# Feature attention in a two-layer decoder kernel: next maxima turned behind the tenth head, values written by GpSimd from a feature-major context, selu added by GpSimd a turn later

## The reference

```python
x = x + _L0_xattn_ref(_layernorm(x, axis=-1), ctx_2048, ctx_2048, L0_xattn_W)

def _L0_xattn_ref(q, k, v, W):          # q, k, v: (32, 64, 256)
    H, D = 8, 8
    SCALE = D ** (-0.5)
    qh = q.reshape(Bq, H, D, Tq); kh = k.reshape(Bq, H, D, Tk); vh = v.reshape(Bq, H, D, Tk)
    a = jnp.einsum('bhdq,bhdk->bhqk', qh, kh) * SCALE
    p = jax.nn.softmax(a, axis=-1)
    y = jnp.einsum('bhqk,bhdk->bhdq', p, vh).reshape(Bq, Cq, Tq)
    out = jnp.einsum('oc,bct->bot', W, y)
    return jax.nn.selu(out)
```

## Time and profile before

| | us |
|---|---|
| median of 3 runs | 1331.83 |
| lowest and highest | 1327.61 and 1333.07 |
| profiled execution, its time | 1335.5 |
| its span | 1333.4 |
| PE busy | 1217.7 (91%) |
| DVE busy | 959.4 (72%) |
| ACT busy | 709.4 (53%) |
| POOL busy | 454.4 (34%) |

### The profile page before, as it was taken

One profiled execution on the slowest core, in us unless ns is written; L12 is line 12 of the kernel. 1 busy time (PEld: TensorE's weight loads), 2 busy tenths in 40 slices (PEclk: granted clock), 3 DMA queues, 4 the chain that ended last, 5 costly groups with the idle time before them and its releaser, 6 DMA issues. The chain is left out here.

```text
span 1333.4 us, 27527 instructions
## 1 busy us (share of the span) xinstructions
PE 1217.7 (91%) x9976; PEld 967.8 (73%) x9976; DVE 959.4 (72%) x1862; ACT 709.4 (53%) x1475; POOL 454.4 (34%) x537
## 2 busy tenths in 40 slices
PE   5999997989888779798899999999997899999998
PEld 3777764444444557697677878788786899999998
DVE  5889987888887376786567778687775668555555
ACT  2778863878778545000466565656653463333332
POOL 2344642454543124575552423323230201112210
PEclk9999998999999988899999999999999999999999
DMA  5111151133331200001300000000000300000001
GB/s 172 36 36 37 42 149 34 41 81 94 80 92 33 74 41 0 1 0 29 119 9 4 4 8 4 8 4 8 4 1 2 95 25 25 25 25 25 1 1 64
DMA packets 58660, 51.04 MB, mean 38 GB/s; under 512 B 9064, under 2 KB 50888, under 8 KB 58184
## 3 DMA queue, kind: packets, MB, share of 16 engines
q1 hardware_dynamic: 58574, 49.88, 13.3%
HBM read 37.93 MB, written 11.53 MB: 37 GB/s over the span
## 5 line engine op out<-in xcount | busy, mean ns | idle before, releaser
L208 DVE TENSOR_REDUCE stacks_neg_max<-psum 128x2 f32<-128x512 f32 x256 | 163.6, 684 | 39.2 <-PE psum L204 38.6
L952 ACT ACTIVATE fa_probs<-psum 128x1024 f32<-128x1024 f32 x128 | 130.3, 1020 | 46.1 <-PE psum L1069 45.3
L1921 PE MATMUL psum<-mo_xT_high,mo_w_high 128*128 128x256 f32 x512 | 145.2, 284 | 2.8 <-DVE mo_xT_low L2755 2.7
L1921 PE MATMUL psum<-mo_xT_low,mo_w_high 128*128 128x256 f32 x512 | 145.0, 283 | 0.0
L1921 PE MATMUL psum<-mo_xT_high,mo_w_low 128*128 128x256 f32 x512 | 144.2, 282 | 0.0
L2587 ACT ACTIVATE mo_silu<-psum 128x256 f32<-128x256 f32 x128 | 49.0, 384 | 155.0 <-PE psum L1921 155.0
L2721 DVE TENSOR_TENSOR mo_mid<-mo_silu,psum 128x256 f32<-128x256 f32 x128 | 53.6, 419 | 92.9 <-ACT mo_silu L2587 92.8
L204 PE MATMUL psum<-stacks_k_stack,stacks_q_stack 48*128 48x256 bf16 x512 | 89.7, 281 | 16.9 <-DVE stacks_neg_max L208 7.8
L2057 POOL TENSOR_TENSOR ga_probs<-ga_probs,ga_top 128x1024 f32<-128x1024 f32 x16 | 30.5, 1905 | 205.4 <-DVE ga_top L2211 205.4
L1921 PEld LDWEIGHTS psum<-mo_xT_high,mo_w_high 128*128 128x128 f32 x512 | 97.0, 189 | 3.2 <-DVE mo_xT_low L2755 2.8
L1921 PEld LDWEIGHTS psum<-mo_xT_low,mo_w_high 128*128 128x128 f32 x512 | 97.1, 190 | 0.0
(11 more groups left out here) (434 smaller groups left out, 3562.3 us busy)
## 6 DMA issues: line engine op xcount, KB each, us to landing
k_parts<-da_k_parts SPq DMA_DIRECT2D x96, 64.0 KB, 2.0
stacks_k_stack<-k_parts SPq DMA_DIRECT2D x32, 192.0 KB
q_parts<-stacks_parts SPq DMA_DIRECT2D x48, 64.0 KB, 2.0
stacks_q_stack<-q_parts SPq DMA_DIRECT2D x32, 96.0 KB
x<-in_x SPq DMA_DIRECT2D x4, 512.0 KB, 7.4
da_context<-in_ctx SPq DMA_DIRECT2D x4, 512.0 KB, 6.9
stacks_q_stack<-q_parts SPq DMA_DIRECT2D x32, 64.0 KB
fa_context<-in_ctx SPq DMA_DIRECT2D x16, 128.0 KB, 2.1
```

The lines of the kernel that those rows point to most:

```text
L208: return core.nc.vector.tensor_reduce(self.neg_max[:, b, :, head_at(h)], core.psum[:, bank, :].rearrange("p (q k) -> p q k", q=2), AX.X, A ...
L952: nc.scalar.activation(probs[:, g].rearrange("p h k q -> p h (k q)"), ps[:, 2 + 2 * (g % 2):4 + 2 * (g % 2), :], ACT.Exp).then_inc(exp_don ...
L1921: done = nc.tensor.matmul(out, lhsT[i], rhs[j], start=start and k == 0, stop=stop and k == 2)
```

## The change

TensorE turns the next tile's maxima of b=0 directly behind `heads(1, 0)`, that is behind head 9, the tenth; it did so behind `heads(1, 1)` and a mix. The `w_out` product moves from there to behind `turn_mixed(t, 0)`, before `heads(1, 3)`, where the two context transposes were. These are gone: SP loads the context from `ctxT`, feature-major, which another sublayer reads already, and GpSimd writes `values` from it by adding zeros. On ScalarE the maxima's rows are copied right after the first exponential of b=1, and `below`, `above` and `exp_below` stand together before the last exponential. On GpSimd selu of tile t-2 comes first in turn t, where that of tile t-1 stood in its middle; `split` moves from first to behind `values_of`. VectorE's `row_stats` moves from behind heads 4 and 5 to behind heads 8 and 9.

```diff
-                sp.dma_start(context[:, slot], dram["ctx"][bass.ts(tile, P), :]).then_inc(context_ready[slot], 16)
+                sp.dma_start(context[:, slot], chunked(dram["ctxT"])[:, :, bass.ts(tile, P)]).then_inc(context_ready[slot], 16)
...
-                        sp.wait_ge(values_psum, t)
+                        sp.wait_ge(values_ready, t)
...
-                        if g == 2 and b == 0 and valid(t - 2):
+                        if g == 0 and b == 1 and valid(t - 2):
                             row_stats(t - 2)
...
                     exponentials(t, 1, 0)
+                if valid(t + 1):
+                    max_to_rows(t + 1, 0)
+                if valid(t):
+                    exponentials(t, 1, 1)
+                    take_mixed(t, 0)
+                    exponentials(t, 1, 2)
                 if valid(t - 1):
                     act.wait_ge(projected, t)
...
-                if valid(t):
-                    exponentials(t, 1, 1)
-                    take_mixed(t, 0)
-                if valid(t + 1):
-                    max_to_rows(t + 1, 0)
...
-                    values_of(t + 1, ring(1))
...
+            def values_of(tile, slot, round):
+                pool.wait_ge(context_ready[slot], 16 * round + 16)
+                if started(tile, RING):
+                    pool.wait_ge(mixed_done, 4 * (tile - 3))
+                as_values = lambda a: a.rearrange("p k (g d) -> p k g d", d=C_HD)
+                nc.gpsimd.tensor_tensor(values[:, slot, :, :, 0:C_HD], as_values(context[:, slot]),
+                                        as_values(zeros[:].rearrange("p (k f) -> p k f", k=KC)), ALU.add).then_inc(values_ready, 1)
...
+                if valid(t - 2):
+                    add_selu(t - 2)
+                if valid(t + 1):
+                    split_max(t + 1, 0)
...
+                    values_of(t + 1, ring(1), rounds(1))
                 if valid(t + 3) and started(t, 1):
                     split(t + 3, ring(3), rounds(3))
...
                 if valid(t + 1):
                     split_max(t + 1, 1)
+                if isinstance(t, int) and t == TILES:
+                    add_selu(t - 1)
...
                 heads(1, 0)
-                if valid(t - 1):
-                    pe.wait_ge(mixed_c_ready, t)
-                    nc.tensor.matmul(ps[:, 7, E:2 * E], w_out[:], mixed_c[:], start=True, stop=True).then_inc(projected, 1)
-                heads(1, 1)
-                if valid(t):
-                    mix(t, ring(0), 0, 1)
...
                     turn_max(t + 1, 0)
+                heads(1, 1)
+                if valid(t):
+                    mix(t, ring(0), 0, 1)
                 heads(1, 2)
                 if valid(t):
                     turn_mixed(t, 0)
-                if valid(t + 1):
-                    pe.wait_ge(context_ready[ring(1)], 16 * rounds(1) + 16)
-                    pe.wait_ge(max_rows_ready, 2 * t + 3)
-                    for k in range(2):
-                        done = nc.tensor.transpose(ps[:, 7, k * P:(k + 1) * P], context[:, ring(1), k * P:(k + 1) * P], ident[:])
-                    done.then_inc(values_psum, 1)
+                if valid(t - 1):
+                    pe.wait_ge(mixed_c_ready, t)
+                    if valid(t + 1):
+                        pe.wait_ge(max_rows_ready, 2 * t + 3)
+                    nc.tensor.matmul(ps[:, 7, E:2 * E], w_out[:], mixed_c[:], start=True, stop=True).then_inc(projected, 1)
```

More of the change, by code:

```diff
@@ L790, in feature_attention @@
         zeros, parts, q_stack, k_stack = stacks.zeros, stacks.parts, stacks.q_stack, stacks.k_stack
-        context = sb("context", [P, RING, E])
+        context = sb("context", [P, RING, KC, P])
         rest = sb("rest", [P, E])
@@ L938, in _ @@
         def _(act):
-            def values_of(tile, slot):
-                act.wait_ge(values_psum, tile + 1)
-                nc.scalar.copy(values[:, slot, :, :, 0:C_HD],
-                               ps[:, 7, 0:E].rearrange("p (k g d) -> p k g d", k=2, d=C_HD)).then_inc(values_ready, 1)
             def max_to_rows(tile, b):
@@ L1037, in split_max, with add_selu @@
                 nc.gpsimd.tensor_tensor(max_parts[:, b, :, :, 2], by_lane(max_rest[:, b]), max_parts[:, b, :, :, 1], ALU.subtract).then_inc(max_split, 1)
-            def turn(t, ring, rounds, valid):
+            def add_selu(tile):
+                pool.wait_ge(exp_below_ready, tile + 1)
+                nc.gpsimd.tensor_tensor(scaled_exp[:], exp_below[:], slope[:].to_broadcast([P, E]), ALU.mult).then_inc(selu_ready, 1)
+                pool.wait_ge(selu_ready, tile + 1)
+                nc.gpsimd.tensor_tensor(negative[:], scaled_exp[:], slope[:].to_broadcast([P, E]), ALU.subtract).then_inc(negative_ready, 1)
+                pool.wait_ge(negative_ready, tile + 1)
+                nc.gpsimd.tensor_tensor(selu[:], above[:], negative[:], ALU.add).then_inc(selu_sum, 1)
+                pool.wait_ge(selu_sum, tile + 1)
+                nc.gpsimd.tensor_tensor(core.x[:, tile, :], core.x[:, tile, :], selu[:], ALU.add).then_inc(x_ready, 1)
@@ new lines, in turn @@
+            def turn(t, ring, rounds, valid):
+                if isinstance(t, int) and t == -1:
+                    pool.sem_inc(split_done, 1)
+                if valid(t - 2):
+                    add_selu(t - 2)
+                if valid(t + 1):
+                    split_max(t + 1, 0)
+                    if isinstance(t, int) and t == -1:
+                        clear_values()
+                        pool.wait_ge(cleared_values, 2)
+                    values_of(t + 1, ring(1), rounds(1))
@@ L1040, in turn @@
                 if valid(t + 3) and started(t, 1):
                     split(t + 3, ring(3), rounds(3))
-                if isinstance(t, int) and t == -1:
-                    pool.sem_inc(split_done, 1)
-                if valid(t + 1):
-                    split_max(t + 1, 0)
-                if isinstance(t, int) and t == -1:
-                    clear_values()
-                if valid(t - 1):
-                    pool.wait_ge(exp_below_ready, t)
-                    nc.gpsimd.tensor_tensor(scaled_exp[:], exp_below[:], slope[:].to_broadcast([P, E]), ALU.mult).then_inc(selu_ready, 1)
-                    pool.wait_ge(selu_ready, t)
-                    nc.gpsimd.tensor_tensor(negative[:], scaled_exp[:], slope[:].to_broadcast([P, E]), ALU.subtract).then_inc(negative_ready, 1)
-                    pool.wait_ge(negative_ready, t)
-                    nc.gpsimd.tensor_tensor(selu[:], above[:], negative[:], ALU.add).then_inc(selu_sum, 1)
-                    pool.wait_ge(selu_sum, t)
-                    nc.gpsimd.tensor_tensor(core.x[:, t - 1, :], core.x[:, t - 1, :], selu[:], ALU.add).then_inc(x_ready, 1)
@@ L1128, in turn @@
                 if valid(t):
-                    pe.wait_ge(values_ready, t + 1)
+                    if valid(t - 2):
+                        pe.wait_ge(channels_read, t - 1)
+                    elif isinstance(t, int) and t == 0:
+                        pe.wait_ge(max_rows_ready, 1)
                     turn_max(t, 1)
```

12 lines of the change are left out of this document (3 added, 9 removed).

## The result

| | before | after |
|---|---|---|
| median, us | 1331.91 (4 runs) | 1318.28 (4 runs) |
| lowest and highest | 1327.61 and 1333.07 | 1313.53 and 1319.73 |
| profiled execution, its time | 1335.5 | 1319.73 |
| its span | 1333.4 | 1317.8 |

The ratio is 0.9897, 95% interval 0.9873 to 0.9922: 13.6 us faster, where 6.6 was forecast, and outside the range. Two later comparisons, each with runs of before on its own chip, gave 0.9895 and 0.9898.

The account below looks back on a forecast made before the run. The prediction took a ring through VectorE and TensorE to bound the kernel. 13 passages gain 7.15, less 0.55 at the ends, giving 6.6 off the median 1331.83: 1325.2 us, range 1320 to 1334.

Parts of the forecast that it names:

- Bound and removed stops: A ring through VectorE and TensorE sets the turn; two of its four stops are waits for something late.
- 0.49 later w_out, 0.70: Before head 14: w_out follows turn_mixed's start by 0.49 and takes 0.70, replacing transposes of 0.31; head 14 at 361.11, not 360.72.
- stop of 0.27 before head 14: VectorE finishes dividing at 361.27 but head 14's result comes at 361.54, a new stop of 0.27.
- w_out is free before head 14: Rival, chance 0.18: the divide is later or the next mix absorbs head 14's delay; 3.8 comes back, 1321.4.
- as the sum is a difference, I take it from the median: Last step of the sum: the 6.6 gain is subtracted from the median of 1331.83, giving 1325.2.
- The lock: VectorE's normalise after heads 0 and 1 is held by selu's first GpSimd instruction until 0.14 after its end; cost 0.02.
- starting over at full length: Skill's rule for the held normalise: full time after 364.62, ending 364.97, 0.22 late, 2.4 us over 11 turns: 1327.6.
- Split earlier by row_stats: Behind head 9: without row_stats before the seventh maximum, the eighth ends 0.3 earlier and GpSimd's split is over at 357.07.
- ScalarE: Three reads in one row before the last exponential delay it to 362.01 to 363.03, leaving 0.18 before TensorE's mix.
- The forecast's sign of being wrong: TensorE's mix behind head 1 names ScalarE for more than 0.2 a turn, or the period stays at 13.6.
- Selu's order: Before head 2: with selu no longer ahead of GpSimd's max split, turn_max comes at 364.10 instead of 364.68.

Follow-up runs that it names:

- values_back: Changed kernel with values written as before: TensorE transposes the context between turn_mixed and w_out, ScalarE copies it; 1321.86 us, ratio 0.9918.
- after_padded_timed: Changed kernel plus 26 unread one-column TensorE matmuls at the end of feature attention, timed beside the changed kernel on one chip; 1321.03 us, ratio 0.9919.
- after_timed: Changed kernel once more with nothing altered, as partner on the same chip; 1318.54 us, ratio 0.9898.
- values_moved_only: Kernel before with only the values' move: context feature-major, GpSimd writes values, TensorE's transposes and ScalarE's copy gone; 1328.59 us, ratio 0.9964.
- after_padded: Changed kernel plus 26 unread one-column TensorE matmuls at the end of feature attention; by its profile feature attention 224.7 us, last stage 301.6.
- before_padded: Kernel before plus 26 unread one-column TensorE matmuls at the end of feature attention; 1328.05 us, ratio 0.9987.
- stats_back: Changed kernel with row_stats back behind heads 4 and 5; one profile, 142.7 us over 11 turns instead of 142.0.
- selu_same_turn: Changed kernel with selu of tile t-1 back in its own turn, between split and split_max of b=1; 1374.44 us.

## Why the prediction was right and wrong

**Bound and removed stops: right.** The stop before head 0 fell from 0.75 to 0.26 (forecast near 0.4), that before head 2 vanished, turn_max of b=0 waits 0.50 for GpSimd (0.5), the one before head 8 grew to 0.56 (0.59), and head 10 to w_out stand within 0.04 of the forecast.

**The term that was mis-sized in the stage: "0.49 later w_out, 0.70".** The 0.71 of the earlier trace rows was read from w_out's start to the next head, with bf16 heads on both sides. The weight loads, before and then after (in the turns of the earlier trace rows and of TensorE's rows above):

```profile
356.58 0.30 PEld L1150 LDWEIGHTS psum<-fa_mixed_c,fa_w_out 128*128 128x128 f32 x2 [0.21 <-issue]
```

```profile
340.44 0.30 PEld L1172 LDWEIGHTS psum<-fa_mixed_c,fa_w_out 128*128 128x128 f32 x2
```

Before, it began only with w_out itself and TensorE had loaded nothing for 0.21; after, it follows turn_mixed's load and begins 0.11 ahead of its matmul, and head 14 follows w_out after 0.53. The load's lead is 0.11 of the 0.18. The rest was there only in the eight turns of the loop: in the turns outside it w_out took 0.63 or 0.64 before (288.12 to 288.76), and after the change it takes 0.53 in either; why the loop's turns had 0.08 more is not shown. Of the forecast's stop of 0.27 before head 14 about 0.1 is left, too little for a bracket: the maximum starts 0.30 behind fa_mixed's start (341.20 to 341.50), where it started 0.20 behind it before (361.15 to 361.35). So 0.17 more a turn is won, 2.2 over 13 turns. The rival "w_out is free before head 14" had part of the outcome, 3.8 where 2.2 came, but not the reason: neither was the divide late nor did the mix take the delay up; the step itself is shorter there. values_back, with 0.22 more in that place, shows such a stop, 0.24.

**The step that failed altogether: "as the sum is a difference, I take it from the median".** It assumed that the rest of the program keeps its time. The change takes rows out of TensorE's program, which no term priced, and shifts its 16 KB loads against the starts of later stages: 2.7 in the last stage by the profiles, 2.5 by the timed comparison of after_padded_timed with after_timed. values_moved_only has the same 2.7 in its last stage, with no gain in its turns; timed it is 3.0 (its median to that of before), or 4.8 (1.9 to 7.7) by its ratio.

**The account of 13.6.** Eleven turns give 7.8; from the second start of head 8 in the stage to the last, 13 passages, it is 9.5 (177.47 before, 167.93 after), where the forecast had 7.15. The whole stage is 8.3 shorter in the first profile and 10.8 in after_timed, which differ by the clock at the start. Profiles with the same mean granted clock over the stage's first 24 us agree better: at 0.64 the stage takes 233.8 in before and 224.7 in after_padded, 9.1 less, and at 0.72 it takes 232.9 in before_padded and 223.0 in after_timed, 9.9 less. With 2.7 for the load that makes 11.8 to 12.6 of the 13.6, whose own interval is 10.4 to 16.9. Whether the shorter stage 4 of the first profiles belongs to the change too stays open.

**The lock: right, by its row.** In the turn shown the normalise ran from 344.25 to 345.02, ending 0.15 behind GpSimd's instruction:

```profile
344.26 0.61 POOL L1029 TENSOR_TENSOR fa_scaled_exp<-fa_exp_below,fa_slope 128x256 f32<-128x256 f32 x1 [0.27 <-issue]
```

That is the 0.14 of the earlier trace rows. But this turn is the exception: it lies between the loop's two rounds, costs 0.25 (13.12 against 12.87), and that is the 0.3 over the stage; it is one turn, not the four of the expectations. In the other turns with selu the normalise starts 0.30 behind GpSimd's instruction, also ends 0.15 behind it, and takes 0.45 to 0.47 (0.46 at 331.38), a hold of 0.05. The Trainium skill's rule (SBUF — State Buffer, section Who interferes with whom) agrees with the row in that the one engine is held by the other; starting over at full length, which I had derived from it, would have ended at 345.27 and is not what the row shows.

**Split earlier by row_stats: right but empty.** The 0.3 that the eighth maximum gained is worth 0.06 a turn (stats_back).

**ScalarE: right.** The last exponential starts at 342.03 and ends at 343.06, 0.12 ahead of the mix at 343.18, a margin of 0.18 forecast. TensorE's matmuls never name it there; the weight load of that mix does, idle for 0.21, which is also what other mixes' loads are idle for without it (10.8 in 50, put down to issue). The forecast's sign of being wrong, over 0.2 a turn, can't be told from that; values_back, with 0.42, shows what a late exponential looks like. **Selu's order: not priced.** The prediction counted 0.29 for head 2; behind it stood a far larger debt, which selu_same_turn shows, since in the new order split fills GpSimd up to 340.9.

## What to carry to other kernels

Find the engine ring that sets a loop's period and lay out every event of one turn; it predicts a reordering to a few hundredths, except that here a float step's length depended on whether its weight load could begin ahead of it, so price a moved step by rows with the same neighbours as it will have. When a change adds or removes instructions ahead of other stages, compare the unchanged stages one by one, since a program load may have moved into or out of their first DMAs, and the clock may follow. And compare periods, not whole stages: a stage's length carries the granted clock of its start, here up to 2.6 us between two profiles of one kernel.

## What the runs showed of the hardware

- One 16 KB instruction load among the first weight DMAs of a stage: one SyncE DMA row takes 0.98 to 1.95 instead of 0.43 to 0.47, the first weights come 1.0 to 1.8 later, TensorE's granted clock over the stage's first 12 us is 0.86 instead of 1.00, and the stage is 2.5 to 3.3 longer. 26 matmuls of one column placed where TensorE idles move it in or out.
- With VectorE stopped for 2.37 before head 2 and 1.54 before head 8, TensorE was granted 0.76 of its clock, and a turn of 12.9 became 16.7.
- Two float steps in a row on TensorE take 1.02 to 1.07, where 0.49 and 0.71, read without a float step ahead of either, add up to 1.20.
- A normalise of 0.40 was held by a GpSimd instruction of 0.61 until 0.15 behind its end, whether it had started with it (0.77) or 0.30 behind its start (0.45 to 0.47).
